# Layer 0 of a two-layer attention and feed-forward kernel: the rounded rows of the ternary product are made bfloat16 by GpSimd and turned as bfloat16

## The reference, cut to what matters

```python
scale = jnp.maximum(act_scale, 1e-05)
x_int = jnp.clip(jnp.round(x / scale), -QB, QB)        # QB = 127
x_dq = jnp.nan_to_num(x_int * scale, ...)
w = ternary_weight.astype(jnp.float32) - 1.0
return jnp.einsum('bsi,oi->bso', x_dq, w) + bias
...
x = x + _L0_xattn_ref(_layernorm(x, axis=-1), ...)
x = x + _L0_ffn_ref(_layernorm(x, axis=-1), ...)
x = x + _L1_xattn_ref(_layernorm(x, axis=-1), ...)
x = x + _L1_ffn_ref(_layernorm(x, axis=-1), ...)
```

## Time and profile before

| | |
|---|---|
| three runs | 1343.40, 1343.62, 1346.10 us; median 1343.62 |
| the profiled execution | 1344.6 us, of which 1342.9 us are the span |
| busy share of the span: PE, DVE, ACT, POOL | 93%, 76%, 65%, 38% |
| mean granted clock of TensorE | 0.97 of full |

### The profile page before, as it was taken

How to read it: one execution, slowest core, us unless ns; L and a number is a source line. 1 busy time by engine, 2 the same in 40 slices (tenths; PEclk the granted TensorE clock), 3 DMA queues, 4 the chain that set the end, 5 groups by cost and what they waited for, 6 DMA issues and landing times. The chain is left out here.

```text
span 1342.9 us, 21702 instructions
## 1 busy us (share of the span) xinstructions
PE 1242.2 (93%) x7683; PEld 648.3 (48%) x7687; DVE 1023.6 (76%) x1756; ACT 868.0 (65%) x1483; POOL 515.3 (38%) x678
## 2 busy tenths in 40 slices
PE   8999899999999999999999999999998999970498
PEld 5566423334343433434555545545554785430298
DVE  5867688898878788886766788888774564996764
ACT  4455437677777777677665655665554666869693
POOL 3555401145343444535565433333334102647600
PEclk9999969999999999999999999999999999995699
DMA  8999774323334242433434553343201001326133
GB/s 270 378 345 330 270 179 111 101 65 104 98 103 131 70 129 80 116 93 105 121 88 108 151 175 96 105 122 87 76 18 48 1 0 47 141 94 240 72 111 110
DMA packets 88074, 170.82 MB, mean 127 GB/s; under 512 B 14742, under 2 KB 49310, under 8 KB 86430
## 3 DMA queue, kind: packets, MB, share of 16 engines
q1 hardware_dynamic: 87083, 167.37, 39.7%
q10 hardware_dynamic: 883, 2.05, 0.7%
HBM read 108.26 MB, written 60.31 MB: 126 GB/s over the span
## 5 line engine op out<-in xcount | busy, mean ns | idle before, releaser
L1391 DVE TENSOR_REDUCE b_neg_max<-b_score 128x1 f32<-128x512 f32 (+3 forms) x864 | 541.3, 663 | 150.3 <-PE b_score L893 75.8
L1136 ACT ACTIVATE b_probs<-b_exp 128x512 f32<-128x512 f32 (+1 forms) x864 | 465.7, 581 | 275.9 <-PE b_exp L917 275.1
L890 PE MATMUL b_score<-b_k_stack,b_q_stack 97*128 97x512 bf16 (+3 forms) x1024 | 356.3, 352 | 10.8 <-DVE b_neg_max L1391 4.9
L917 PE MATMUL b_exp<-b_q_stack,b_k_stack 100*128 100x512 bf16 (+3 forms) x1024 | 344.5, 341 | 5.9 <-ACT b_probs L1136 5.6
L938 PE MATMUL b_av<-b_probs,b_values 128*17 128x512 f32 (+3 forms) x2048 | 228.6, 518 | 3.9 <-POOL b_probs L1234 3.6
L890 PEld LDWEIGHTS b_score<-b_k_stack,b_q_stack 97*128 97x128 bf16 x1024 | 99.8, 98 | 247.6 <-DVE b_neg_max L1391 130.0
L917 PEld LDWEIGHTS b_exp<-b_q_stack,b_k_stack 100*128 100x128 bf16 x1024 | 100.2, 98 | 78.7 <-ACT b_probs L1136 22.6
L1234 POOL TENSOR_SCALAR_AFFINE_SELECT b_probs<-b_probs 128x512 f32<-128x512 f32 x96 | 61.7, 643 | 169.9 <-ACT b_probs L1136 169.4
L1250 POOL CAST b_max_parts<-b_neg_max 128x16 bf16<-128x16 f32 x64 | 12.9, 202 | 274.5 <-DVE b_neg_max L1391 272.9
L893 PE MATMUL b_score<-diag_qk,minus_big 128*128 128x128 bf16 x512 | 112.7, 220 | 0.0
L1677 PE MATMUL f_bank<-normed,f_w_upT 128*128 128x512 f32 x192 | 82.7, 592 | 0.0
(11 more groups left out here) (250 smaller groups left out, 2120.5 us busy)
## 6 DMA issues: line engine op xcount, KB each, us to landing
b_q_stack<-s_q SPq DMA_DIRECT2D x378, 64.0 KB
s_k<-a_part_k SPq DMA_DIRECT2D x48, 256.0 KB, 3.3
b_k_stack<-s_k SPq DMA_DIRECT2D x60, 192.0 KB
s_up<-f_up SPq DMA_DIRECT2D x6, 1536.0 KB, 5.0
s_va<-a_va SPq DMA_DIRECT2D x16, 544.0 KB, 5.5
b_values<-s_va SPq DMA_DIRECT2D x16, 544.0 KB, 4.5
a_mask_q<-mask_in SPq DMA_DIRECT2D x8, 1024.0 KB, 8.0
b_k_stack<-s_k SPq DMA_DIRECT2D x60, 128.0 KB
```

What stands on the lines that cost most here:

```text
L890: mm = pe.matmul(o, q, KS[half][0:R_MAX, h, 0:w], start=True, stop=causal or not general)
L917: mm = pe.matmul(o, k, QS[half][0:NSTACK, h, q0:T], start=True, stop=not masked)
L1136: nc.scalar.activation(probs[kc][:, h0:h0 + m, q0:T], exp_bank[n % RINGS][:, 0:m * w].rearrange("p (h n) -> p h n", h=m), ACT.Exp).then_in ...
L1391: nc.vector.tensor_reduce(neg_max[u][:, qt, h0:h0 + m], score_bank[n % RINGS][:, 0:m * w].rearrange("p (h n) -> p h n", h=m), AX.X, ALU.ma ...
```

## The change

GpSimd makes a third pass over the rounded rows: it adds -MAGIC to XN and writes the integers as bfloat16 to a new place XQ, in the free half of the row that holds XQT. The turns of j = 2 take XQ instead of XN, with the bfloat16 identity, and write bfloat16 to PSUM (the same bank read as bfloat16). ScalarE's copy to XQT has no bias any more. `quantized` now counts three passes a batch, and the turns wait for the third. The new pass waits for the turns of the batch before, since they read XQ. The bias constant and its memset are gone.

```diff
--- before.py
+++ after.py
@@ -633,7 +633,6 @@
         var = sb("var", [P, TT], F32)
         less_half = sb("less_half", [P, TT], F32)
         less_mean = sb("less_mean", [P, TT], F32)
-        less_magic = sb("less_magic", [P, 1], F32)
         part = ffn.turned_to["down"][:, :, :].rearrange("p f d -> p (f d)").bitcast(BF16).rearrange("p (i c n) -> p i c n", i=PARTS, c=DC)
 
         SPLITS = ['wo0', 'wo1']
@@ -647,6 +646,8 @@
         XB, XN, XN2, X2 = (room(i, TT) for i in (1, 2, 3, 4))
         XT, full = (room(i, DC) for i in (5, 6))
         XQT = normed[:, 7, 0:TT * D // 2].bitcast(BF16).rearrange("p (c n) -> p c n", c=DC)
+        XQ = normed[:, 7, TT * D // 2:TT * D].bitcast(BF16).rearrange("p (t d) -> p t d", t=TT)
+        work_b = work[:, :].bitcast(BF16)
 
         preset, rows_set, key_rows_set = sem("preset"), [const["rows_set"], sem("rows_set1")], [const["key_rows_set"], sem("key_rows_set1")]
         stack_landed = [[sem(f"stack_landed{i}{g}") if i or g else const["stack_landed"] for g in range(G)] for i in range(2)]
@@ -678,7 +679,7 @@
         RING = 2 * G
         LEAD = RING - 1
         STEPS = 4 * TT
-        PRESETS = 3
+        PRESETS = 2
         ROWS_SET = 16
         NLOADS = 10
         SLOTS = range(-2, LAST + 10)
@@ -1021,8 +1022,9 @@
                         mm = product_of_parts(attT_high, attT_low, f"wo{l}", n - 2, out)
                     elif n < 6:
                         if n == 4:
-                            pe.wait_ge(quantized, 2 * (b + 1))
-                        mm = turn(XN, n - 4)
+                            pe.wait_ge(quantized, 3 * (b + 1))
+                        for x in range(TT):
+                            mm = pe.transpose(work_b[:, x * P:(x + 1) * P], XQ[:, x, (n - 4) * P:(n - 3) * P], const["ident_b"][:, :])
                     else:
                         mm = product(XQT, w["tern"], n - 6)
                     mm.then_inc(after_full[l], 1)
@@ -1099,7 +1101,7 @@
                 if l == 0 and j == 2 and s in (3, 7):
                     c = s // 4
                     act.wait_ge(after_full[0], NF[0] * b + c + 5)
-                    nc.scalar.activation(XQT[:, c, :], work[:, :], ACT.Identity, bias=less_magic[:, 0:1]).then_inc(by_act[0], 1)
+                    nc.scalar.activation(XQT[:, c, :], work_b[:, 0:T], ACT.Copy).then_inc(by_act[0], 1)
 
             def queries(b, j, s):
                 if j == 1 and s in (3, 7):
@@ -1203,8 +1205,12 @@
                 if j == 1 and kc == 2:
                     pool.wait_ge(ln_out[0], TT * (NLN[0] * b + 1))
                     nc.gpsimd.tensor_scalar(XN, XN, 127.0, -127.0, ALU.min, ALU.max).then_inc(quantized, 1)
-                    pool.wait_ge(quantized, 2 * b + 1)
+                    pool.wait_ge(quantized, 3 * b + 1)
                     nc.gpsimd.tensor_scalar(XN, XN, MAGIC, None, ALU.add).then_inc(quantized, 1)
+                    if b > 0:
+                        pool.wait_ge(after_full[0], NF[0] * (b - 1) + 6)
+                    pool.wait_ge(quantized, 3 * b + 2)
+                    nc.gpsimd.tensor_scalar(XQ, XN, -MAGIC, None, ALU.add).then_inc(quantized, 1)
                 if j == 3 and kc == 1:
                     root(0, NLN[0] * b + 1)
                     normalize(XN2, X2, 5 * b + 5)
@@ -1286,7 +1292,6 @@
         def _(dve):
             nc.vector.memset(av_bank[:, :], 0.0).then_inc(preset, 1)
             nc.vector.memset(less_half[:, :], -0.5).then_inc(preset, 1)
-            nc.vector.memset(less_magic[:, :], -MAGIC).then_inc(preset, 1)
             ffn.begin()
 
             def moments(l, b, x, m, j, s):
```

## The result

The changed kernel takes 1352.71 us (median of six runs, 1348.81 to 1354.6), against 1344.03 for the kernel before, run beside it; the ratio is 1.0056, interval 1.0046 to 1.0066, or 7.5 us slower (the two medians are 8.7 apart; what follows goes by the ratio). The forecast was 1347.3, 3.7 us slower, with a range to 1348.6: slower, as said, but twice as much. The profiled execution is one of the quick ones, 1350.97 us with a span of 1349.2.

The account below looks back on a forecast made before the run. TensorE's queue was taken to set the pace in the slot of the change. Hidden batches -1.8, batch 0 +2.6 and batch 7 +2.9 gave +3.7 us on 1343.6, so 1347.3, with a range from 1343.2 to 1348.6.

Parts of the forecast that it names:

- The pass, 2.79 us from the row of its own form: GpSimd's new pass in each batch priced like the MAGIC-adding pass, 2.79 us, plus 0.09 between dependent passes: 2.88.
- Hidden in batches 1 to 6: Layer 0's attention: the pass fits GpSimd's idle before the maxima's split, costs nothing; each batch gains 0.3, -1.8 us.
- The turns, 0.4 a batch and 0.3 of it arriving: TensorE's bfloat16 turns save 0.2 us a group, 0.4 a batch; waiting for ScalarE leaves 0.3.
- partly made up: Rival, chance 0.13: stalls let VectorE's and ScalarE's waits vanish once each, turns may give 0.4 a batch; +2.2 us, 1345.8.
- Batch 0, +2.6: TensorE already waits for GpSimd before batch 0's turns, so the pass is exposed: +2.88 - 0.3 = +2.6 us.
- Batch 7, +2.9: In layer 1's slots GpSimd's chain to the second cut, needed by the weighing, moves by 2.88 whole; faster turns gain nothing.
- The sum without the clock, +3.7: Whole kernel: -1.8 for batches 1 to 6, +2.6 for batch 0, +2.9 for batch 7, giving +3.7 us.
- The clock: Rival, chance 0.05: TensorE's idles in batches 0 and 7 drop it to 1.2 GHz once, up to 12 us, 1359.

Follow-up runs that it names:

- e8: Changed kernel with its third GpSimd pass made a copy of the low 16 bits, read as integers, to bfloat16; ratio 0.9993 to the kernel before.
- e10: Kernel before plus the third pass in all eight batches, output unread, float32 turns waiting for it, copy with bias kept; one execution, 1354.12 us.
- e3: The change in batches 1 to 6 alone, batches 0 and 7 as in the kernel before; ratio 0.9989 to the kernel before.
- e2: Kernel before plus the third pass in batches 0 and 7 alone, output unread, float32 turns waiting for it; ratio 1.0053 to the kernel before.
- e11: Changed kernel with ScalarE's copy back in its old form, an identity with a bias, here zero; one execution, 1350.30 us.
- e1: Changed kernel with eleven matmuls on constants ahead of TensorE's wait for the third pass in batches 0 and 7; 1346.68 us, ratio 1.0015 to before.
- e7: Changed kernel, second and third GpSimd passes fused and cut in halves, split of layer 1's output weight one slot later; ratio 0.9994 to before.

## Why the prediction was right or wrong

- **The pass, 2.79 us from the row of its own form:** right, 2776 ns. The Trainium skill (GPSIMD Engine Reference, Engine selection) calls one-input work "roughly line-rate". Set beside the 1041 ns row, that holds here for the copy in e8 (1037 ns) and for min and max, and fails for an addition of a constant, 2776 to 2789 ns.
- **Hidden in batches 1 to 6:** right. The turns of batch 1 start 0.9 us behind the pass, as worked out, and e10 puts the cost at 0.0 us.
- **The turns, 0.4 a batch and 0.3 of it arriving:** the term was a little small. They save 0.47 and 0.37 arrives. Batches 1 to 6 give 2.14 in the trace of e3, and 2.49 in the changed kernel, where a wait of 0.35 us behind batch 1 is gone too. The prediction had that as "partly made up", by the stalls. The stalls are not what does it: e2, e10 and e11 have them and keep the wait. Why it goes in some traces and not in others is open.
- **Batch 0, +2.6:** 2.35 where the clock stays (e1), so a little less.
- **Batch 7, +2.9:** right where the clock stays, 2.88 in e1, the whole length of the pass, so the faster turns gain nothing there. The reason given was right too: in e1 the weighing of slot 35 starts 0.10 us behind GpSimd's cut (699.13 and 699.23), as before, and e7 loses nothing in that slot. Under the lower clock it is different. In the changed kernel the cut ends at 699.29 and the weighing starts only at 700.92, so TensorE's own stream is the longer one, and there the new turns do gain: with 3.4 us at 0.50 each, the old turns cost 3.99 and 3.97 us there (e2, e10) and the new ones 3.58 (e11).
- **The sum without the clock, +3.7:** about 1 us too high, 2.70 in the trace of e1 and 2.0 in its timed runs (0.7 to 3.2). Most of it is the gain of the hidden batches, 2.5 in place of 1.8.
- **The clock:** this step failed. It stood as a rival with a chance of 0.05 and a price of 12 us, with an idle of 2.17 us that did no harm and one of 4.75 that did. I read the space between as mostly harmless and took the price of a fall from the one long stretch at hand. The runs show both wrong. In the traces of the changed kernel, e2, e10 and e11, with idles of 2.97 to 3.53 us, the clock fell at both places, eight times of eight; and a fall costs 0.7 to 1.6 us, not 12, since it lasts 3.4 or 6.8 us. In the trace the two falls are 3.2 us; by the ratios of the timed runs, taking them away gives back some 5.5, of which 2 are not explained.
- **The mistake in one sentence:** the fall of the clock was treated as a case that may come or not, while it belonged to the sum as a term, since each stall of 3 us on the busy TensorE of this kernel brought it.

## What to carry to other kernels

A pass that hides in the steady state of a pipeline must be costed at its first and last round on its own: six batches hid it for nothing, and the two ends paid more than the six had gained. Where TensorE sets the pace, price a stall of 3 us as its length plus a stretch at half clock behind it, and when such a stall can't be avoided, matmuls on constants in the wait give that second part back (22 matmuls here: 3.2 us in the trace, some 5.5 by the timed ratios). When work is moved away from one wait, look for the wait ahead of which it lands: e7 gave back in slot 36 what it had won in slot 35. On GpSimd, take a pass's price from a row with the same operation, not the same shape.

## What the runs showed of the hardware

- The granted clock fell for 3.4 or 6.8 us behind idles of TensorE of 2.97 to 3.53 us each time (eight). Behind shorter ones it fell or not: it did after 2.28 and 1.77 us, it did not after 1.71, 1.82 and 2.61, and at the two idles of 1.57 to 1.67 us near 1040 us it did 2 times of 26. I had not expected the short ones.
- GpSimd on 1024 elements a partition: min and max with constants 1041 ns, copy of 16-bit integers at a stride of two to bfloat16 1037, one addition of a constant 2776 to 2789, two additions 3663 ns. I had expected the step from one to two operations, and not from one kind to another, to count.
- At the full granted clock, four bfloat16 turns of 128 by 128 take 0.22 or 0.23 us of TensorE's stream, four float32 ones 0.43 or 0.49.
